# When GpSimd issues the 21 gathers of a scan step: in one row, or three at a time behind pieces of the adjacency matrix

## What is computed

```python
h = relu(layernorm(x))
wh = (h @ weight).reshape(n, 4, 32)
e = leaky_relu(parent_logit[:, None, :] + child_logit[None, :, :], 0.2)
att = softmax(where(adj > 0, e, -9e15), axis=1)
x = x + einsum('njh,jhf->nhf', att, wh)
h = relu(layernorm(x))
msg = relu((adj @ h) @ W_msg.T + b_msg)
x = x + gru_cell(msg, h, W_ih, W_hh, b_ih, b_hh)
```

## Time and profile before

| | us |
|---|---|
| median of 3 runs | 981.84 |
| lowest, highest run | 980.51, 986.42 |
| the profiled execution, from its first to its last instruction (its span) | 1278.8 |
| in it, the last adjacency piece done by ACT | 958.2 |
| in it, busy: PE, DVE, ACT, POOL | 730.5, 744.5, 654.5, 508.6 |

### The profile page before, as it was taken

The page is one execution under the profiler, slowest core; times in us unless marked ns, Lnnn a source line. Parts: engine busy times, 40 slices in busy tenths (PEclk is TensorE's granted clock), DMA queues, the critical chain, the costliest instruction groups (busy, mean ns, idle before and its releaser), DMA issues.

```text
span 1278.8 us, 12294 instructions
## 1 busy us (share of the span) xinstructions
PE 730.5 (57%) x3331; PEld 439.4 (34%) x3381; DVE 744.5 (58%) x3128; ACT 654.5 (51%) x667; POOL 508.6 (40%) x518
## 2 busy tenths in 40 slices
PE   2665447374764747647372726363736454329987
PEld 1443224142432424324141414141414342106643
DVE  7577438484774847748472819383846451127754
ACT  2767518293774937748381809191923122005532
POOL 3110461433426234262435261727255447730360
PEclk9878767685877768777685767676767577659998
DMA  9999928685977969878684858686810002211121
GB/s 318 421 420 423 415 98 344 263 364 209 418 315 297 377 250 415 324 292 349 269 367 145 359 202 334 236 335 233 328 36 19 26 25 51 52 37 34 53 71 34
DMA packets 55750, 305.51 MB, mean 239 GB/s; under 512 B 13825, under 2 KB 31442, under 8 KB 39296
## 3 DMA queue, kind: packets, MB, share of 16 engines
q1 hardware_dynamic: 27936, 274.74, 52.9%
q0 software_dynamic: 17152, 23.15, 6.7%
q10 hardware_dynamic: 10592, 6.82, 1.8%
HBM read 295.65 MB, written 12.71 MB: 241 GB/s over the span
## 4 chain that ended last, share of the span: by engine, by line
another core or an unknown queue 29%; DVE 27%; PE 20%; ACT 11%; issue 8%; DMA 4%; POOL 1%; ACTq 0%; DVEq 0%; POOLq 0%
ACT ind L666 7%; PE ps L925 4%; DVE cand L1389 3%; DVE list_arena L1565 3%; DMA x<-in_x 2%; PE ps L1137 2%; PE ps L970 1%; DVE rows_in L1505 1%; PE ps L971 1%; PE ps L972 1%; PE ps L1160 1%; PE ps L904 1%; PE ps L1162 1%; PE ps L1161 1%
## 5 line engine op out<-in xcount | busy, mean ns | idle before, releaser
L666 ACT ACTIVATE ind<-adj_in 128x4096 bf16<-128x4096 int32 x128 | 461.8, 3608 | 18.1 <-PE ps L925 6.6
L925 PE MATMUL ps<-ind,bit_w 128*128 128x512 bf16 x993 | 318.2, 460 | 194.2 <-ACT ind L666 161.1
L557 POOL DMA_INDIRECT val<-in_adj,val_idx x144 | 151.7, 1054 | 421.7 <-DVE val_idx L1599 351.0
L925 PEld LDWEIGHTS ps<-ind,bit_w 128*128 128x128 bf16 x1024 | 114.5, 114 | 366.5 <-ACT ind L666 175.1
L1389 DVE MAX8 cand<-ps 128x8 f32<-128x256 f32 x256 | 91.1, 418 | 197.2 <-remote 184.3
L539 POOL DMA_INDIRECT rows_in<-wh_table,idx x180 | 180.9, 1005 | 62.3 <-issue 62.3
L617 POOL DMA_INDIRECT adj_in<-g_table,idx x96 | 93.6, 975 | 105.5 <-PE ps L1139 69.3
L694 ACT COPY pm<-ps 128x32 f32<-128x32 f32 x16 | 3.0, 185 | 233.2 <-remote 232.6
L970 PE MATMUL ps<-rows_in,ident 128*128 128x132 f32 x120 | 37.7, 412 | 59.3 <-DVE rows_in L1505 59.2
L957 PE MATMUL ps<-pm,own 128*128 128x8 f32 x128 | 24.5, 320 | 73.0 <-issue 58.9
L1719 DVE TENSOR_SCALAR adj_in<-iota,edge_row,val 128x128 f32<-128x128 f32 x128 | 34.2, 346 | 47.6 <-remote 33.8
(11 more groups left out here) (299 smaller groups left out, 1586.2 us busy)
## 6 DMA issues: line engine op xcount, KB each, us to landing
adj_in<-in_adj SPq DMA_DIRECT2D x128, 2048.0 KB
wh_table<-rows_in POOLq DMA_DIRECT2D x16, 264.0 KB, 8.5
g_table<-t_buf ACTq DMA_DIRECT2D x16, 256.0 KB
out<-rows_in SPq DMA_DIRECT2D x16, 256.0 KB
rows_in<-wh_table,idx POOLq DMA_INDIRECT x180
val<-in_adj,val_idx POOLq DMA_INDIRECT x144
adj_in<-g_table,idx POOLq DMA_INDIRECT x112
ind<-g_table,idx POOLq DMA_INDIRECT x16
```

What stands on the lines that cost most here:

```text
L557: nc.gpsimd.indirect_dma_start(out=val2[:, s, k:k + 1], out_offset=None, in_=adj_values, in_offset=bass.IndirectOffsetOnAxis(ap=val_idx2[: ...
L666: nc.scalar.activation(ind[:, (tile * 2 + half) % IND, :], adj_in[:, slot, 0:b - a].bitcast(I32), ACT.Relu, bias=1.0, scale=-1.0, accum_ou ...
L925: ins = nc.tensor.matmul(o, bit_w[:, b, :], ind[:, (tile * 2 + half) % IND, c0:c0 + HALF], start=False, stop=(b == BITS - 1))
```

## The change

In a scan step POOL now issues the rows of group s before the values of group s-1, no longer after them, and it waits between them: a helper `piece(s, n)` waits until ACT has done piece 8(s+1)+n. The 12 row gathers go in four portions of three, behind four successive pieces; the 9 value gathers in three portions of three, behind the three pieces after those. The wait is capped at the last piece, 128. Group 0's rows and the values of groups 14 and 15 have no such wait.

```diff
+                def piece(s, n):
+                    pool.wait_ge(ind_done, min((s + 1) * 2 * G + n, 2 * T))
+
                 def rows(s):
                     if s >= 2:
                         pool.wait_ge(agg_mm, s - 1)
                     pool.wait_ge(idx_done, s + 1)
                     pool.sem_inc(passed_pool, 1)
                     for t in range(G):
+                        if s >= 1:
+                            piece(s, 5 + t)
                         for k in range(3):
                             nc.gpsimd.indirect_dma_start(
...
                 def values(s):
                     pool.wait_ge(idx2_done, s + 1)
                     for k in range(E2):
+                        if s < NG - 2 and k % 3 == 0:
+                            piece(s + 1, 9 + k // 3)
                         nc.gpsimd.indirect_dma_start(
...
                 rows(0)
                 for s in range(1, NG - 1):
+                    rows(s)
                     values(s - 1)
-                    rows(s)
                     if s == FIRST_SCAN:
```

## The result

| | before | changed |
|---|---|---|
| median of 18 runs, us | 976.97 | 985.02 |
| lowest, highest | 969.72, 986.42 | 978.65, 996.19 |
| ratio, 95% interval | | 1.0073 (1.0051 to 1.0096) |

The change makes the kernel 0.7% slower: 988 was forecast against a median of 981.84, that is +6.6 us, and it is about +7 to +8. The ratio is formed from the fast runs alone, so it is not the quotient of the two medians. The time is right; a good part of the reading of the profile before is not, as the next rows show.

A forecast was written before the change was run, and what follows sets the result against it. The prediction took the stream of pieces at 423 GB/s as mostly bounding the timed scan, late PE signals the profiled execution. Scan 0 and tail +6.6 on 981.84 gave 988 us; its own range 981 to 992, for 8 in 10 953 to 997.

The forecast's parts named there:

- PE's signals come late while POOL issues gathers in a row, and that bounds it: Whole profiled execution: 371 us of the span are late signals, at most 74 us of them left in a timed run.
- Scan 0: In the scan: bytes and rate stay the same, so spreading the gathers gives 0 if the stream bounds.
- The end of the scan: POOL's queue behind the last piece: gathers held for it make POOL 6.6 us late, reaching the end whole; bounds 0 and 8.9.
- T0: The end of ACT's last piece in the scan, 958.24 us in the first trace; times at the end count from it.
- Before, T0 + 14.0: End of the scan, kernel before: start of the last group's rows in a timed run, against T0 + 20.6 after the change.
- the row's 11.7: End of the scan: in the first trace the last group's first indices came at T0 + 11.7, making POOL 8.9 us late.
- the 2.3 us allowed for DVE: Last tile of the scan: DVE's search would start 6.1 us after its piece in a timed run, not 3.9.
- Hidden, barely: DVE at L1470 comes at about T0 + 40, just behind the last group's rows, which end at T0 + 37.0.
- POOL is what comes last: Tail, ahead of the last values: without late signals POOL's 19.3 us of idle time goes, so 6.6 us reach the end.
- A: Rival, scan: late signals are in timed runs and portions of three don't cause them; 963 us if half real, 938 all; chance 0.30.
- B: Rival, end of scan: late signals are real but POOL's total counts, not its rows; +14.4 us, 996 us; chance 0.17.
- C: Rival, scan: pieces come unevenly and portions bunch to 6 or 9 gathers; 988 us again; chance 0.53 together with the forecast.

The follow-up runs named there:

- the clean profile: The kernel before, unchanged, profiled a second time: span 974.0 us, timed 975.84 us in the same execution.
- e7: The kernel before with portions of three behind pieces only for rows of groups 1 to 9 and values of groups 0 to 8; 1.0009 of before.
- the third execution: The kernel before, unchanged, profiled a third time: span 975.9 us, timed 977.68 us in the same execution.
- e3: The kernel before with rows of group s ahead of values of group s-1 in every step, no wait added; 1.0083 of before.
- e2: The kernel before with only the last step of the loop as in the changed kernel, the scan in rows of 21 gathers; 1.0124 of before.
- e15: The changed kernel with group 13's nine values behind the last group's row gathers instead of ahead of them; 1.0112 of before.
- e8: The changed kernel with the four early rows of group 10 moved behind the last nine value gathers; 1.0046 of before.
- e14: The kernel before with the four early rows of group 10 moved behind the last nine value gathers; 970.1 us, 0.9951 of before.
- e10: The kernel before with early rows of group 9 ahead of the last group's rows, those of group 10 behind the last values; 0.9975 of before.

## Why the prediction came out as it did

**What bounds the kernel.** Wrong as the trace was read, right where it was not trusted. The step "PE's signals come late while POOL issues gathers in a row, and that bounds it" describes one odd execution. (One reading in it is off: in the earlier trace rows ACT goes on 2.6 us after POOL's last gather, 463.64 and 466.24, not a little over 1.) The correction made from the times (908 us without them, the median only 74 us above, so mostly the stream bounds a timed run) was right: the clean profile has the stream as 36% of the chain and a DMA share of 1.01 in the scan. A gap between span and run as large as 297 us is no property of the profiler either. In each profiled execution whose own time is on record the run is 1.8 to 1.9 us longer than the span (975.84 and 974.0 in the clean one); that of the first profile isn't on record. The Trainium skill (Runtime: NRT & Kernel Launch, The ~15µs preamble/postamble breakdown) puts the total of a profile some 6 us above the reported time, the same for every kernel. Here the span, from the first to the last instruction, lies 1.8 to 1.9 us below the time instead: steady, but on the other side. The rule's real use would have been as an alarm: a profile that lies 297 us off the runs is not a profile of those runs.

**Scan 0.** Right: e7 gives 1.0009 (0.9969 to 1.0049) for groups 1 to 9, and the windows of before and of the changed kernel have 406 and 404 GB/s.

**The end of the scan.** The place is right, POOL's queue behind T0, and the delay reaches the end whole: 11.1 us at the last rows, 11.1 at the last values, 10.8 at the edge gathers. The size, 6.6 us, and part of the reason are not. "`rows_of_last` starts at T0 + 20.6" came out as 22.7, because the last portion starts 0.9 us behind the piece and single gathers last up to 2.1 us. "Before, T0 + 14.0" rested on a POOL that idles 18.5 us until the first indices of group 15. The clean profile has no such idle time: the indices are there at T0 + 9.3, and nine gathers of POOL's own queue set the 11.6. So the row's 11.7, kept as the other bound, agrees with it by luck, and the 2.3 us allowed for DVE have no ground: its search of the last tile begins 2.2 us behind T0 (3.6 in the third execution), not 6.1. The reason was too narrow as well. It charged the 16 gathers that "can't start before T0"; e3, where nothing waits for a piece, already has 7.8 of the 11.1 us, from the order alone.

Timed, the whole change costs 8.05 us between medians (5.0 to 9.4 by the interval), e2 alone 12.9 (7.3 to 16.9). The 10.8 us between the two timelines, or 9.6 against the third execution, lie just above the first interval and inside the second, and where the rest goes is not shown. That the forecast of 6.6 lies so near the timed figure, with a term that the timelines have at 10 to 11, is in part luck.

**Who waits.** "Hidden, barely" for DVE at the last rows was wrong: it waits 6.5 us for them in the changed kernel, which the prediction had named as a sign of being wrong. e15 shows that this doesn't set the end, since the last values come later still. "POOL is what comes last", through the edge test at PE, was right, and e8, e14 and e15 show it in both directions.

**The rivals.** A fell with e7. B needed late signals; e2 had 16 gathers behind the last piece, and DVE's search of the last tile, which waits for PE's words, began 2.2 us behind T0 (748.24 and 750.43), as in the clean profile of before (754.50 and 756.70). In the changed kernel it began 3.9 us behind, far from the 10 that B asked for; PE's eight products for that tile took 3.60 us there and 1.90 in the clean profile of before, at a granted clock of 0.50 (762 to 766 us, the lower of its two levels, 1.2 GHz) and 1.00 (754 to 758 us, the upper). C happened in part: in the changed kernel nine row gathers ran together at 518.6 to 530.1, since their indices came at 517.8, behind the first of the pieces they wait for, and each of the next two pieces was done before POOL had finished the three gathers ahead of it. As said, this changed nothing.

**What would show it.** The span "perhaps 1100 to 1200" was wrong, and "a profiled gain that the timed runs don't have is the mark of the forecast" came true for the wrong reason: the odd execution was on the side of before. The signs for the tail came, POOL without a pause from T0 + 0.9 and the last group's rows at T0 + 22.7. The idle time before the last values is gone too, but the clean profile of before hasn't got it either.

## What to carry to other kernels

When the span of a profile lies far from the timed runs, profile again before reading it; the difference of two clean timelines, both counted from the same event, then tells in a few microseconds what a change does. A queue worked off in order needs its deadline looked at where the work runs out, not in the steady part: here the 21 gathers a body of groups 1 to 9 could go in rows or in portions for free, and 8 to 11 us of delay in POOL's queue at the end cost about 1%. The order alone can make such a delay: of two jobs in a queue, the one whose inputs are ready first was put second. Moving the gathers that nobody awaits behind the ones that gate the next stage is worth half a percent with one line.

## What the runs showed that was not expected

One profiled execution of three of the same program had a span of 1278.8 us instead of 974.0 and 975.9. In it ACT waited at L694 for 15 signals of PE, up to 26.0 us, and went on in twelve of the cases 2.6 to 4.2 us after a row of POOL's gathers had ended. No other profile here, with rows of 21 gathers (e2, e3, e10, e14) or portions, showed it again. What set it off wasn't found, and since it didn't come back it could not be tried; that the gathers held the signals up is not shown.
